# A two-layer attention and expert network on one core: rows 0 and 1 of the delta rule's lead-in interleaved on TensorE, and the field attention's tail moved by rows

## The reference, cut to what matters

```python
q = l2norm(silu(h @ Wq)); k = l2norm(silu(h @ Wk)); v = silu(h @ Wv)
beta = sigmoid(h @ Wb)
alpha = exp(-exp(A_log) * softplus(h @ Wa + dt_bias))
for each token t:
    S = S * alpha_t
    S = S + k_t (x) ((v_t - k_t S) * beta_t)
    o_t = q_t S * scale
x = x + (rms_norm(o) * w * silu(h @ Wg)) @ Wo
```

## Time and profile before

| | |
|---|---|
| runs shown | 1925.17, 1921.43, 1924.22 us; median 1924.22 |
| profiled execution's own time | 1930.55 us |
| its span | 1928.8 us |
| mean granted TensorE clock | 0.908 |
| TensorE busy | 1637.9 us, 85% |
| VectorE busy | 1256.8 us, 65% |
| ScalarE busy | 1075.3 us, 56% |
| GpSimd busy | 865.0 us, 45% |

### The profile page before, as it was taken

One profiled execution on the slowest core, in us unless ns is written; L12 is line 12 of the kernel. 1 busy time (PEld: TensorE's weight loads), 2 busy tenths in 40 slices (PEclk: granted clock), 3 DMA queues, 4 the chain that ended last, 5 costly groups with the idle time before them and its releaser, 6 DMA issues. The chain is left out here.

```text
span 1928.8 us, 42957 instructions
## 1 busy us (share of the span) xinstructions
PE 1637.9 (85%) x15415; PEld 1172.2 (61%) x15415; DVE 1256.8 (65%) x3303; ACT 1075.3 (56%) x3164; POOL 865.0 (45%) x1080
## 2 busy tenths in 40 slices
PE   0799828994349975999989889999999999899988
PEld 0345417994239972666557767777777777566633
DVE  7586644554344537787776867777777777467757
ACT  0353303442124432888885567777777777777653
POOL 0235673664646651334332877607062534532223
PEclk9996758996569995999999989999999999999989
DMA  2940013423112225000002322222212132221001
GB/s 68 384 137 23 23 45 101 122 79 107 55 54 73 73 89 170 23 28 22 22 20 84 93 66 57 60 65 65 73 40 73 44 78 59 70 53 35 28 12 44
DMA packets 157666, 135.73 MB, mean 70 GB/s; under 512 B 90021, under 2 KB 130279, under 8 KB 155303
## 3 DMA queue, kind: packets, MB, share of 16 engines
q1 hardware_dynamic: 146950, 113.91, 20.1%
q0 software_dynamic: 9088, 18.70, 3.0%
q10 hardware_dynamic: 1440, 0.66, 0.1%
HBM read 76.65 MB, written 56.54 MB: 69 GB/s over the span
## 5 line engine op out<-in xcount | busy, mean ns | idle before, releaser
L848 POOL DMA_INDIRECT y<-moe_y,moe_aim x156 | 177.7, 1139 | 142.8 <-DVE moe_y L988 62.1
L2870 DVE TENSOR_TENSOR delta_sv<-delta_sv,delta_zp 32x256 f32<-32x256 f32 x384 | 161.3, 420 | 114.2 <-PE delta_zp L2443 106.7
L1810 ACT ACTIVATE field_p<-field_sp,field_nm 128x128 f32<-128x128 f32 x512 | 180.2, 411 | 1.5 <-DVE field_nm L1901 1.0
L2783 POOL TENSOR_TENSOR delta_dd<-delta_dd,delta_prod 128x30 f32<-128x30 f32 (+11 forms) x270 | 160.3, 594 | 21.1
L2781 POOL TENSOR_TENSOR delta_prod<-delta_ll,delta_dd 128x30 f32<-128x30 f32 (+11 forms) x270 | 144.9, 537 | 21.2
L2776 POOL TENSOR_TENSOR delta_dd<-delta_ll,delta_minus 128x1024 f32<-128x1024 f32 (+1 forms) x9 | 23.3, 2584 | 275.1 <-DMA delta_ll<-lanes 275.0
L1810 ACT ACTIVATION_READ_ACCUMULATOR field_p<-field_sp,field_nm 128x1 f32 x512 | 128.3, 251 | 0.0
L2443 PE MATMUL delta_zp<-delta_sv,delta_ct 128*32 128x128 f32 x1536 | 122.5, 280 | 4.6 <-DVE delta_sv L2870 4.3
L2854 DVE SCALAR_TENSOR_TENSOR delta_la<-delta_xp,delta_ck,delta_dc 128x256 f32<-128x256 f32 x256 | 107.6, 476 | 9.0 <-PE delta_xp L2401 7.4
L1911 DVE COPY field_pT<-field_ptp 128x512 f32<-128x512 f32 x128 | 84.0, 672 | 36.9 <-PE field_ptp L1660 36.9
L2443 PEld LDWEIGHTS delta_zp<-delta_sv,delta_ct 128*32 128x32 f32 x1536 | 70.2, 109 | 56.6 <-issue 25.0
(11 more groups left out here) (574 smaller groups left out, 4472.8 us busy)
## 6 DMA issues: line engine op xcount, KB each, us to landing
delta_al<-alpha SPq DMA_DIRECT2D x33, 512.0 KB, 4.5
pairs<-c_none SPq DMA_DIRECT2D x16, 1032.0 KB, 16.3
moe_xg<-pairs SPq DMA_DIRECT2D x78, 129.0 KB
moe_yt<-y SPq DMA_DIRECT2D x16, 512.0 KB, 4.7
w_E<-in_E_dram SPq DMA_DIRECT2D x1, 4624.0 KB, 36.7
w_E<-in_E_dram SPq DMA_DIRECT2D x8, 578.0 KB, 4.0
lanes<-delta_la SPq DMA_DIRECT2D x256, 16.0 KB, 1.5
delta_di<-inverses SPq DMA_DIRECT2D x64, 64.0 KB, 2.3
```

Of the source, the lines that this page charges most:

```text
L848: nc.gpsimd.indirect_dma_start(results, bass.IndirectOffsetOnAxis(ap=aim[:, t % AR, j:j + 1], axis=0), y[:, t % YS, j, :], None).then_inc( ...
L1810: last = nc.scalar.activation(p[:, slot, h, :], s_ps[i][:, k, :], ACT.Exp, bias=nm[:, slot, h:h + 1], accum_out=zs[:, slot, h:h + 1])
L2783: last = nc.gpsimd.tensor_tensor(dd[lanes, a + 1:, 0:a], dd[lanes, a + 1:, 0:a], pr, ALU.subtract)
L2870: nc.vector.tensor_tensor(sv[rows, two, :], sv[rows, two, :], z_ps[2 * pair // HH][rows, at, :], ALU.subtract).then_inc(s["z_kept"], 1)
```

## The change

It has five parts. On VectorE the 8 copies of `diagonal` are made two at a time behind the four sequences of group 6, no more in one piece behind group 7; `alpha_size(0)` is done behind sequence 0 of group 7, not 1. On SyncE `load_first(0)` is issued ahead of `load_alpha` of row 3, and the store of group 7's norm goes from row 2 to row 3. On TensorE the projections of rows 0, 1 and 2 are cut in halves: half of row 1 is made ahead of row 0's norms, the rest and half of row 2 behind row 0's key products, the rest of row 2 behind row 1's key products. The gate logits of group 7, its root and the second alpha turn are made one row later. On ScalarE group 7's factors are kept behind row 0's four quarters, and the second half's exponential, logarithm and decay come one row later. On VectorE the tails follow by one row, except `alpha_sum(1)` and `alpha_out(1)`, which stay.

```diff
@@ field attention, VectorE
                     keep_turned(n, now, 3)
-                    if final and b == 1:
+                    if isinstance(it, int) and half == 0:
+                        diagonal(ch, range(2 * b, 2 * b + 2))
+                    if final and b == 0:
                         alpha_size(0)
...
         norm_before(B, 1)
-        diagonal(ch)
         alpha_sum(0)
@@ delta rule, SyncE
                     store_lanes(Row(0, k))
+                    if k == GB // 2 - 1:
+                        load_first(0)
                     if k + 2 <= AHEAD:
                         load_alpha(Row(0, k + 2))
-                    if k == GB // 2 - 1:
-                        load_first(0)
-                    if k == GB // 2:
+                    if k == GB - 1:
                         store_norm()
-                    if k == GB - 1:
                         load_first(1)
@@ delta rule, TensorE
-                def project_ahead(p, before={}):
+                def project_ahead(p, some):
                     pe.wait_ge(hk_in[p.half], p.two * 16 + 16)
-                    for i in range(4):
+                    for i in some:
                         if p.n * 4 + i > 1:
                             pe.wait_ge(s["pre_kept"], p.n * 4 + i - 1)
-                        if i in before:
-                            before[i]()
...
-                project_ahead(Row(0, 0), {2: spread_and_turn, 3: factors_last})
+                project_ahead(Row(0, 0), range(2))
+                spread_group(GROUPS - 1)
+                alpha_turn(0)
+                project_ahead(Row(0, 0), range(2, 4))
+                factors_last()
+                project_ahead(Row(0, 1), range(2))
                 pe.wait_ge(fs["y_kept"], GROUPS + 1)
                 for k in range(AHEAD + 1):
                     p = Row(0, k)
                     norms(p, k > 0)
                     if k == 0:
                         output_last()
+                    if 1 < k < AHEAD:
+                        project_ahead(Row(0, k + 1), range(4))
                     if k < AHEAD:
-                        project_ahead(Row(0, k + 1), {2: lambda: norm_columns(p)} if k == 0 else {})
+                        norm_columns(p)
                         if k == 0:
                             pe.wait_ge(fs["peak"], SCORED)
                             pe.wait_ge(fs["al_out"], 1)
-                        else:
-                            norm_columns(p)
                         for i in range(2):
                             if k:
                                 pe.wait_ge(s["la_kept"], 2 * k + i - 1)
                             key_products(p, i, k == 0)
                         if k == 0:
+                            project_ahead(Row(0, 1), range(2, 4))
+                            project_ahead(Row(0, 2), range(2))
+                        if k == 1:
                             alpha_beta_last()
-                        if k == 1:
+                            project_ahead(Row(0, 2), range(2, 4))
+                        if k == 2:
                             spread_group(GROUPS)
-                        if k == RING - 3:
+                        if k == RING - 2:
                             alpha_turn(1)
@@ delta rule, ScalarE
                                              z_ps[i % 2][:].rearrange("p h t -> p (h t)"), ACT.Silu).then_inc(s["pre_kept"], 1)
+                    if 4 in before:
+                        before[4]()
                     if p.n < AHEAD:
                         load_keys(Row(0, p.n + 2))
...
-                    keep_ahead(Row(0, k), {2: (keep_factors_last, keep_sum_last)[k]} if k < 2 else {})
-                    if k == 3:
+                    keep_ahead(Row(0, k), ({4: keep_factors_last}, {2: keep_sum_last})[k] if k < 2 else {})
+                    if k == 4:
                         alpha_exp(1)
-                    if k == 4:
+                    if k == 5:
                         alpha_ln(1)
-                    if k == 5:
+                    if k == 6:
                         alpha_last(1)
@@ delta rule, VectorE
-                def diagonal(links):
-                    for h in range(H):
+                def diagonal(links, heads):
+                    for h in heads:
...
-                    if k == 0:
+                    if k == 1:
                         keep_logits_last()
-                    if k == 1:
+                    if k == 2:
                         scale_last()
                         alpha_size(1)
-                    if k == 2:
+                    if k == 3:
                         norm_rows_last()
-                    if k == 3:
                         alpha_one(1)
```

More of the change, by code:

```diff
@@ L2579, in _ @@
                 pe.wait_ge(fs["vm_made"], SPREAD)
-                def spread_and_turn():
-                    spread_group(GROUPS - 1)
-                    alpha_turn(0)
-                project_ahead(Row(0, 0), {2: spread_and_turn, 3: factors_last})
+                project_ahead(Row(0, 0), range(2))
[4 more added lines that the diff above has]
+                project_ahead(Row(0, 1), range(2))
                 pe.wait_ge(fs["y_kept"], GROUPS + 1)
```

## The result

The changed kernel takes 1916.73 us (median of 20 runs, 1911.54 to 1927.20), the one before 1925.32 beside it (20 runs, 1917.93 to 1928.01). The ratio is 0.9969, with a 95% interval of 0.9959 to 0.9979: 6.0 us faster (4.0 to 7.9), where 12.9 was forecast. The medians lie 8.6 apart, and the runs of the changed kernel spread over 16 us, those of before over 10. That spread turned out to be a part of the answer. The profiled run is the slowest of the 20: span 1925.4, 1927.20 with what lies around it.

What follows compares the result with a forecast made beforehand. GpSimd's inversions, started when the first lanes land, were taken to bound the row loop, with a clock loss in the last field group second; 5.6 - 0.8 + 7.0 + 1.1 = 12.9 off 1924.2 gave 1911.3 us, range 1906 to 1918.

Steps and rivals of the forecast that it cites:

- Step 1: Field attention's last group: decay sizes one row earlier end ScalarE's 3.63 us wait and keep TensorE's clock; gain 5.6 us.
- Step 2: Group 6 on VectorE: the eight diagonal copies cost 0.4 us behind rows 0 and 2 each, 0.8 us in sum.
- Rival B: Last field group: its gain is not realised because TensorE or VectorE holds the group anyway; 1916.9 us, chance 0.10.
- Steps 3 and 4: Lead-in: row 1's keys end 7.0 us earlier; SyncE loading lanes ahead of alpha gains 1.1 us.
- From the first projection to GpSimd's start: Lead-in sign: first delta projection to GpSimd's first inversion takes 35.3 us instead of 43.4.
- The keys of row 1: Lead-in sign: they end 17.7 us after row 0's norm products begin, instead of 23.6.
- Five long GpSimd operations in the first half: GpSimd's inversions: five of VectorE's scans lie in the first half, each lengthening one GpSimd operation by 1.9 us.
- rival A: GpSimd held by a sixth scan, or TensorE at 1.2 GHz in row 1, about 2 us; 1913.2 us, chance 0.14.
- Step 5: Other rows and tail: the tail one row later removes ScalarE's waits, but GpSimd covers TensorE's gain; 0 us.
- The stand before row 0: TensorE's wait for the inverses ahead of the delta rule's row 0: still 7 to 9 us.
- Rival E: Tail: TensorE, ScalarE and VectorE wait for each other in a ring, up to 9.6 us per stage; 1940 us, chance 0.03.
- the cover by GpSimd's inversions: Rows 3 to 6 in e7: 3 to 7 us more waiting hidden behind GpSimd's inversions, time as e4.

Runs made afterwards that it cites:

- e1: Kernel before with only the decay sizes moved from behind row 1 to behind row 0 of the field's last group: ratio 0.9972, 5.4 us faster.
- e4: Changed kernel with only the diagonal's copies put back behind the last group: ratio 0.9937 to the kernel before, 12.1 us faster.
- e2: Kernel before with only the eight diagonal copies moved, two at a time, behind the rows of group 6: ratio 1.0035, 6.7 us slower.
- e3: Changed kernel with both field attention edits (decay sizes, diagonal) undone, leaving lead-in, SyncE's order and tail: ratio 0.9969 to the kernel before, 6.0 us faster.
- e11: Changed kernel with only row 2's pair of diagonal copies moved, behind VectorE's product v in row 3: ratio 0.9917 to the kernel before, 16.0 us faster.
- e7: e4 with ScalarE's tail and TensorE's turn of alpha one row earlier: ratio 0.9981 to the kernel before, 3.7 us faster; 8.4 slower than e4.
- e13: e4's kernel run again, beside e11 on one chip: ratio 0.9923 to the kernel before, 14.8 us faster.
- e9: Changed kernel with two diagonal copies each behind rows 1 and 3 of group 6, four behind the last group: ratio 0.9930 to the kernel before.

## Why the prediction failed

The step that failed is the second, the cost of the copies: forecast 0.8 us, measured some 6. The rest of the sum came out in kind.

**Step 1, the decay sizes: right.** Forecast 5.6, measured 5.4 alone (e1, 1.5 to 9.2), 5.4 in group 7's length too (33.3 to 27.9). The push of y by 0.8 is there: TensorE waits 1.13 instead of 0.37.

**Step 2, the copies: this failed.** The step read: "Behind rows 1 and 3 VectorE is idle soon after ..., behind rows 0 and 2 others wait for it: twice 0.4", 0.8 in sum and 2.05 at most. They cost 6.1 (e4 against the full change) to 6.7 (e2) in the timed runs; from group 6 to row 4 the three profiles of the changed kernel take 13.1, 3.0 and 2.7 us more than e4's. I bounded the price by the length of the copies; the bound has to hold what a stand of TensorE does to its clock, which I had weighed in step 1 (low clock, 2.6 us) and not here. I also took 0.4 for each pair without asking what GpSimd does beside it, though the trace of before had a copy of 0.87 us beside a GpSimd operation, where the median copy takes 0.22 (under group 6). Rival B has the time, 1916.9, and the median of 1916.7 lies in the stated range, but that is luck: B's reason was that TensorE or VectorE holds group 7 anyway, and e1 shows that they do not.

**Steps 3 and 4, the lead-in: right in kind, 2 short.** Forecast 7.0 and 1.1, measured 6.0 for both (e3, 3.7 to 8.5, so 8.1 is not excluded by the time alone). In e3's profile GpSimd starts 6.8 us closer to the projection, and 1.3 of it go again between its second half and row 0 (8.5 us instead of 7.2). From the first projection to GpSimd's start 36.0 to 37.0 us were seen in the thirteen profiles with this lead-in and order, 35.3 forecast. The keys of row 1 end 19.3 us after row 0's norms begin, not 17.7: the key products of row 0 take 3.66, as the earlier trace rows had it, where I put 2.4, so the rest of row 1 starts later. The order on SyncE is worth 0.6 at GpSimd's start and nothing measurable in the time, not 1.1. I had priced it by the inverses' landing "with nothing ahead", which was misread: the same 512 KB of alpha were issued 3.2 us ahead of their store. Five long GpSimd operations in the first half: as forecast, so the sixth of rival A stayed away. Its other half, row 1 at the low clock, is not in this profile but in the five named under e11, at 1.7 us for the key products.

**Step 5, the tail: no loss, but not for the reason given.** The stand before row 0 kept its 7 us and row 4 its 2. e7 shows that the distance is needed with the new lead-in: one row less on ScalarE and TensorE costs 8.4. No run has the whole old tail beside the new lead-in. Rival E, the ring, was the right mechanism to fear; I put it off with margins, and the cover by GpSimd's inversions that I expected in e7 does not exist.

Put together: 5.4 - 6.1 + 6.0 + 0 = 5.3, measured 6.0. The forecast without the copies, 13.7, stands against 12.1 for e4.

## What to carry to other kernels

Work moved beside a busy TensorE is not priced by its own length: ask whether TensorE will stand for it, if only for 0.5 to 0.9 us, and put the low clock (3 to 10 us here) into the bounds. When one place costs that, moving the same work behind the operation that TensorE waits for can give it back (e11 is no slower than e13, which has no copies there). And a stand that ends with a DMA is cover only as far as what is queued ahead of that DMA's issue allows.

## Not expected of the hardware

- One program with the same stands in group 6 to 0.01 us has its low clock for 10.3, 3.3 and 3.3 us in group 6 (from the mean clock of its windows), and for some 19 us or not at all in group 7.
- From the start of GpSimd's second half to row 0 on TensorE the profiles give 7.0 to 7.4 or 8.1 to 8.7 us but for one of 7.7 (e9) and the 22.3 of e7, in the kernels with the old lead-in as well (7.2, 7.3 and 8.4). In the changed kernel the 512 KB of alpha were issued on the same queue 2.1 us before the inverses' store, in the kernel before 3.2 us; the placing load could be issued 4.3 us after the store began instead of 3.3. e1 (1.0 and 4.4) and e4 (3.5 and 3.3) go the same way. That the one causes the other was not tried.
